# Eight buffers instead of four for the streamed weights in the last stage of a transformer layer

## The chip, the cores and the metric

One Trainium2 chip, all 8 of its cores. Each core runs the same program on its own half of one of the four sequences. The time is the device time of the slowest core, in microseconds (us). In the views, PE is TensorE (its matmuls), PEld its weight loads, DVE is VectorE, ACT is ScalarE, POOL is GpSimd and SP is SyncE. SPq, POOLq and so on are the instruction queues of these engines, out of which DMAs are issued too.

## The reference

`x` is `[4, 2048, 2048]`. The layer is attention and then a feed-forward block, each behind a layer norm and added to `x`. What is computed in the stretch that the change touches is the second half of the feed-forward block:

```python
h = value * jax.nn.silu(gate)        # [4, 2048, 8192]
h = _bitlinear(h, w_out)             # h rounded to -127..127 per row, w_out [2048, 8192] to -1, 0, 1
return residual + h
```

`_bitlinear` rounds the activation by its row's largest value and the weight by its mean absolute value, then multiplies. So the last product is, for each core, `[1024, 8192] x [8192, 2048]` on small whole numbers held as bf16, followed by a scale per row and the addition of the residual.

## The kernel before

The program is a row of blocks with a full barrier between two of them (`fence_block`: SP waits for every counter). The blocks are: constants, projections, attention, the first part of the feed-forward, the gate and value product (`p5_gv`), the rounding and transposing of `w_out` into a DRAM scratch `TOUT` (`p6_tout`), and at last `p7_out2`, the product with `w_out`.

`TOUT` holds the ternary `w_out`, transposed, in bf16 as `[16, 64, 128, 128]`: 16 blocks of 128 output columns, 64 blocks of 128 rows of the contraction.

`p7_out2` runs three blocks, b = 0, 1, 2. The core's 1024 rows are two halves of four row tiles (`qt` 0 to 3).

- With b = 0 and b = 1 it builds (`bld`): it loads the hidden activation from `HMID`, rounds it on DVE, transposes it on PE and puts it at `AQ2T` in SBUF.
- With b = 1 and b = 2 it multiplies (`mm`) the half that was built in the block before. With b = 2 it only multiplies.

The multiplication goes over `j` (0 to 3, 512 output columns each) and inside it over `oc` (0 to 63, the contraction). One step, `("MM", j, oc)`, is a group of four matmuls of 128x128 by 128x512, one for each `qt`, which add into the four banks of `PS_SC`. The right-hand side is a tile of `TOUT`, 128 partitions by 512 columns of bf16 (128 KB), and it is loaded anew for each group: 256 loads in the block, in pieces of 256 bytes (`tob_load`, L1522 to L1532). With `idx = j * 64 + oc` the tile goes into buffer `idx % 4`, at `TOB + (idx % 4) * 256`, and is announced by semaphore `TSEM[idx % 4]`. SP issues the load as soon as the group `idx - 4`, which read that buffer last, has ended (L1526). PE waits for the semaphore at L1637 and runs the four matmuls at L1642.

After group 63 of a `j`, DVE makes four output tiles, `("yb", j, qt)`: it waits for the group, for a tile of the residual (`AF<-X1scr`, two buffers) and for the store from two steps earlier (two buffers `YB`), and then runs L1604 and L1608. POOL stores each tile (`y<-AF`). The first group of the next `j` waits for `("yb", j, 3)`, since it overwrites the banks.

SP issues everything in one written order: for each `j` the 64 `tob_load`, then the four `x1_load` of that `j`. `x1_load` number `idx2` waits for `yb` number `idx2 - 2` (L1538), so the third and fourth of a `j` wait until this `j`'s first two output tiles are made, and the 64 loads of the next `j` stand behind them.

With b = 1 one transpose step stands ahead of every fourth group, and one `HMID` load ahead of every four `tob_load`.

SBUF from 32768 on (in columns of 4 bytes) holds the work buffers of this stage: `HM2` 32768, `AQN` 36352 and 43776 (256 columns each), `TOB` 36608, `X1B7` 37632, `XH` 38656, `YB` 39680, the rounding buffers `ZP7` 40704 to 43776. What lies at 44032 to 45056 is read no more by then.

Of the kernel before, what the change touches and what calls it, by code (L numbers as in the profile page):

```python
# [30 lines left out]
class Prog:  # L31
# [1418 lines left out]
    def p7_out2(self):  # L1450
# [7 lines left out]
        TOB = 36608  # L1458
# [3 lines left out]
        gp_done = self.cnt["GP"]  # L1462
        st_done = self.cnt["ST"]
        TSEM = ["H0", "H1", "S0", "S1"]

        for b in range(3):
            bld = b <= 1
            mm = b >= 1
            self.fence_block(f"f_p7_{b}")
            c0 = dict(self.cnt)  # L1470
            pe_prog, dv_prog, ac_prog = [], [], []
# [30 lines left out]
            PEn = {op: c0["PE"] + i + 1 for i, op in enumerate(pe_prog)}  # L1502
# [3 lines left out]
            with nc.Block(f"p7_{b}") as blk:  # L1506
                @blk.sync
                def _(sy):
                    if b == 0:
                        sy.wait_ge(self.sems["GP"], gp_done)  # L1510
                        sy.wait_ge(self.sems["ST"], st_done)

                    def hm2_load(k):
                        qt, oc16 = k // 16, k % 16
                        i = b * 4 + qt
                        if k >= 4:
                            sy.wait_ge(self.sems["DV"], DVn[("rnd", k - 4)])
                        self.dma(sy, self.af(HM2 + (k % 4) * 512, 512),
                                 self.HMID.ap()[i * 128:(i + 1) * 128,
                                                oc16 * 512:(oc16 + 1) * 512],  # L1520
                                 f"L{k % 4}")

                    def tob_load(j, oc):
                        idx = j * 64 + oc
                        if idx >= 4:
                            sy.wait_ge(self.sems["PE"], PEn[("MM", (idx - 4) // 64,  # L1526
                                                            (idx - 4) % 64)])
                        vsrc = bass.AP(self.TOUT, (j * 4) * 1048576 + oc * 16384,
                                       [[128, 128], [1048576, 4], [1, 128]])
                        self.dma(sy, self.bap(2 * (TOB + (idx % 4) * 256),  # L1530
                                              [[128, 4], [1, 128]]),
                                 vsrc, TSEM[idx % 4])  # L1532

                    def x1_load(j, qt):
                        i = (b - 1) * 4 + qt
                        idx2 = j * 4 + qt
                        if idx2 >= 2:
                            sy.wait_ge(self.sems["DV"], DVn[("yb", (idx2 - 2) // 4,  # L1538
                                                            (idx2 - 2) % 4)])
                        self.dma(sy, self.af(X1B7 + (idx2 % 2) * 512, 512),  # L1540
                                 self.X1scr.ap()[i * 128:(i + 1) * 128,
                                                 j * 512:(j + 1) * 512],
                                 f"X{idx2 % 2}")

                    if bld and mm:
                        for j in range(4):
                            for kk in range(16):
                                hm2_load(j * 16 + kk)
                                for o4 in range(4):
                                    tob_load(j, 4 * kk + o4)  # L1550
                            for qt in range(4):
                                x1_load(j, qt)
                    elif bld:
                        for k in range(64):
                            hm2_load(k)
                    else:
                        for j in range(4):
                            for oc in range(64):
                                tob_load(j, oc)
                            for qt in range(4):  # L1560
                                x1_load(j, qt)

                @blk.vector
                def _(v):
                    rp_feed, rp_flush = self.rp_pipe(v, ZP7, 512)
                    for op in dv_prog:
# [26 lines left out]
                        else:  # L1593
                            rp_flush()
                            _, j, qt = op
                            i = (b - 1) * 4 + qt
                            idx2 = j * 4 + qt
# [17 lines left out]
                @blk.tensor  # L1615
                def _(te):
                    for op in pe_prog:
                        if op[0] == "T":
                            k = op[1]
                            qt = k // 16  # L1620
                            qtg = b * 4 + qt
                            te.wait_ge(self.sems["DV"], DVn[("rnd", k)])
                            if k >= 2:
                                te.wait_ge(self.sems["AC"], ACn[("evac", k - 2)])
                            psb = (self.PS_C if k % 2 == 0
                                   else self.PS_D).ap().bitcast(BF16)
                            for sub in range(4):
                                _l = te.transpose(psb[:, sub * 128:(sub + 1) * 128],
                                                  self.bap(2 * AQN[k % 2] + sub * 128,
                                                           [[1, 128]]),  # L1630
                                                  self.C_idb.ap())
                            _l.then_inc(self.inc("PE", 1), 1)
                        else:
                            _, j, oc = op
                            idx = j * 64 + oc
                            qtg0 = (b - 1) * 4
                            te.wait_ge(self.sems[TSEM[idx % 4]],  # L1637
                                       c0[TSEM[idx % 4]] + 16 * (idx // 4 + 1))
                            if oc == 0 and j > 0:
                                te.wait_ge(self.sems["DV"], DVn[("yb", j - 1, 3)])  # L1640
                            for qt in range(4):
                                _l = te.matmul(  # L1642
                                    self.PS_SC.ap()[:, qt * 512:(qt + 1) * 512],
                                    self.bap(2 * AQ2T + oc * 1024 + (qtg0 + qt) * 128,
                                             [[1, 128]]),
                                    self.bap(2 * (TOB + (idx % 4) * 256), [[1, 512]]),
                                    start=(oc == 0), stop=(oc == 63))
                            _l.then_inc(self.inc("PE", 1), 1)

# [86 lines left out]
```

## Time and profile before

| | us |
|---|---|
| median of the two runs | 7420.96 |
| the two runs | 7306.04 and 7535.88 |
| the profiled execution | 7303.48 |
| its span on the slowest core | 7301.9 |

The views are all of the profiled execution and of core 0, the slowest. Its times count from the first instruction, so the last instruction stands at 7301.9. "Idle before" is the time in which an engine stood still ahead of an instruction, and what follows the arrow is what ended the wait. PEclk or the granted clock is TensorE's clock as a share of 2.4 GHz; 0.50 is 1.2 GHz.

### The profile page before, as it was taken

What the parts mean: (1) busy time and instruction counts of PE and PEld (TensorE: products, weight loads), DVE (VectorE), ACT (ScalarE), POOL (GpSimd) and SP (SyncE); (2) the same over time, 40 slices, a digit from 0 to 9 for tenths busy, and PEclk for the clock granted to TensorE, in tenths of its full rate; (3) what the DMA queues carried; (4) which work ended last, traced back from release to release, by engine and by line L of the source; (5) the groups of instructions that cost most, each with busy time, mean ns of one, the idle gap of its engine ahead of it and who ended that gap; (6) DMA issues with size and microseconds to landing.
All of it is one profiled execution on the core that took longest, in us unless ns stands there. A gap on an engine that the chain in (4) does not pass through costs nothing. (4 is left out here: it accounts for less than half of the span.)

```text
span 7301.9 us, 63207 instructions; the slowest of 8 cores (7249.2 to 7301.9 us)
## 1 busy us (share of the span) xinstructions
PE 4948.8 (68%) x21575; PEld 2384.2 (33%) x21894; DVE 2250.0 (31%) x2790; ACT 1501.2 (21%) x2439; POOL 367.1 (5%) x620
## 2 busy tenths in 40 slices
PE   1666329997898866686767783488888863336776
PEld 1222114443343333332433331234443432212222
DVE  4100260001101123102232213645555546673300
ACT  4555420000000012101222200222222223310000
POOL 0111000000111100000000000000000000000000
PEclk9887659998998977787888886699999985558899
DMA  6899612111101121212111112433333339835555
GB/s 225 281 322 318 207 58 62 55 48 47 35 33 44 41 64 51 68 60 76 52 47 45 41 59 80 166 123 130 130 130 125 116 119 271 212 103 131 134 122 129
DMA packets 665414, 832.70 MB, mean 114 GB/s; under 512 B 434960, under 2 KB 518032, under 8 KB 608144
## 3 DMA queue, kind: packets, MB, share of 16 engines
q1 hardware_dynamic: 468368, 501.45, 23.0%
q0 software_dynamic: 49792, 268.47, 10.6%
q10 hardware_dynamic: 146944, 58.73, 3.0%
q8 instruction: 184, 3.01, 0.2%
q14 instruction: 126, 1.03, 0.0%
HBM read 702.66 MB, written 125.83 MB: 113 GB/s over the span
## 5 line engine op out<-in xcount | busy, mean ns | idle before, releaser
L1285 PE MATMUL PS_SC<-AF 128*128 128x512 bf16 x2048 | 802.4, 392 | 8.4 <-PEq L1209 1.4
L1279 PE MATMUL PS_SC<-AF 128*128 128x512 bf16 x1929 | 757.7, 393 | 60.0 <-PEq L1209 60.0
L904 PE MATMUL PS_C<-AF 128*128 128x512 f32 (+3 forms) x768 | 406.0, 619 | 324.7 <-ACT AF L984 322.2
L653 PE MATMUL PS_D<-AF 128*128 128x512 bf16 x2257 | 531.0, 394 | 139.3 <-ACT AF L673 136.5
L1642 PE MATMUL PS_SC<-AF 128*128 128x512 bf16 x2002 | 524.5, 411 | 101.6 <-DMA AF<-TOUT 64.6
L653 PE MATMUL PS_C<-AF 128*128 128x512 bf16 x2258 | 528.2, 393 | 89.6 <-ACT AF L673 64.4
L748 PE MATMUL PS_C<-AF 128*128 128x512 bf16 x1506 | 341.9, 385 | 151.1 <-DVE AF L723 149.5
L179 ACT ACTIVATE AF<-AF 128x2048 f32<-128x2048 f32 x192 | 366.4, 1909 | 264.5 <-DMA AF<-wgv 170.8
L653 PEld LDWEIGHTS PS_D<-AF 128*128 128x128 bf16 x2304 | 231.4, 101 | 433.5 <-issue 181.9
L871 PE MATMUL PS_SC<-AF 128*128 128x512 f32 (+1 forms) x640 | 316.7, 632 | 71.1 <-DMA AF<-Qscr 48.6
L616 DVE CAST AF<-AF 128x2048 bf16<-128x2048 f32 x32 | 39.2, 1226 | 1025.4 <-PE PS_D L653 997.1
L653 PEld LDWEIGHTS PS_C<-AF 128*128 128x128 bf16 x2304 | 230.6, 101 | 381.5 <-issue 129.1
L1021 PE MATMUL PS_C<-AF 128*128 128x512 f32 x512 | 248.7, 648 | 132.0 <-DMA AF<-wo 132.0
L748 PE MATMUL PS_D<-AF 128*128 128x512 bf16 x1505 | 334.8, 379 | 1.6
L1642 PEld LDWEIGHTS PS_SC<-AF 128*128 128x128 bf16 x2048 | 200.0, 104 | 400.8 <-issue 253.6
L537 PE MATMUL PS_C<-C_idb,AF 128*128 128x128 bf16 x384 | 56.2, 300 | 389.5 <-DVE AF L496 359.8
L1279 PEld LDWEIGHTS PS_SC<-AF 128*128 128x128 bf16 x2048 | 206.2, 101 | 309.1 <-issue 95.4
L1244 DVE SCALAR_TENSOR_TENSOR AF<-AF,V_sgv 128x2048 bf16<-128x2048 f32 x128 | 301.0, 2352 | 13.4
L924 DVE TENSOR_TENSOR PS_SC<-PS_SC,AF 128x256 f32<-128x256 f32 x128 | 55.4, 433 | 783.4 <-PE PS_SC L871 693.7
L1285 PEld LDWEIGHTS PS_SC<-AF 128*128 128x128 bf16 x2048 | 205.7, 100 | 244.1 <-issue 29.5
L968 ACT ACTIVATE AF<-PS_SC,TMP 128x256 f32<-128x256 f32 (+7 forms) x128 | 156.2, 1220 | 584.5 <-DVE TMP L943 500.9
L1256 DVE SCALAR_TENSOR_TENSOR AF<-PS_SC,C1c,AF 128x512 f32<-128x512 f32 x128 | 96.1, 751 | 556.5 <-ACT AF L1323 540.6
(160 smaller groups left out, 5594.3 us busy)
## 6 DMA issues: line engine op xcount, KB each, us to landing
AF<-wgv POOLq DMA_DIRECT2D x128, 1024.0 KB, 8.4
AF<-wgv SPq DMA_DIRECT2D x128, 1024.0 KB, 4.9
AF<-wout POOLq DMA_DIRECT2D x64, 1024.0 KB, 7.7
AF<-wout SPq DMA_DIRECT2D x64, 1024.0 KB, 7.6
AF<-TOUT SPq DMA_DIRECT2D x512, 128.0 KB, 2.9
AF<-wo SPq DMA_DIRECT2D x128, 256.0 KB, 6.2
HMID<-AF POOLq DMA_DIRECT2D x128, 256.0 KB, 2.6
TOUT<-AF ACTq DMA_DIRECT2D x128, 256.0 KB, 6.2
```

What stands on the lines that cost most here:

```text
L179: sc.activation(buf, buf, ACT.Abs, accum_out=self.PARTS.ap()[:, k:k + 1]).then_inc(self.inc("CR", 1), 1)
L653: _pe_last = te.matmul(ps, self.bap(2 * wb[h % 2] + c * 128, [[1, 128]]), self.bap(2 * xb + c * ncols + grp * 512, [[1, 512]]), start=(c = ...
L748: _pe_last = te.matmul(ps, self.bap(2 * xb + c * ncols + tk * 128, [[1, 128]]), self.bap(2 * (wv_ + c * 256), [[1, 512]]), start=(c == 0 a ...
L871: _l = te.matmul(self.PS_SC.ap()[:, ck * 512:ck * 512 + n], self.af(QB0 + (h % 2) * 512 + qt * 128, 128), self.af(KB0 + (h % 2) * 2048 + c ...
L904: te.matmul(self.PS_C.ap()[:, qlo * 128:512], self.af(VB0 + (h % 3) * 2048 + kt * 128, 128), self.af(PTB0 + (kt % 2) * 512 + qlo * 128, 51 ...
L968: sc.activation(self.af(PB0 + (h % 2) * 8192 + qt * 2048, rng), self.PS_SC.ap()[:, 0:rng], ACT.Exp, bias=self.TMP.ap()[:, 4 + qt:5 + qt], ...
L1021: _pe_last = te.matmul(ps, self.af(AVT + c * 512 + qt * 128, 128), self.af(WOB + c * 512, 512), start=(c == 0), stop=(c == 15))
L1244: v.scalar_tensor_tensor(self.bap(2 * (NTB + (g % 2) * 1024), [[1, 2048]]), w, self.V_sgv.ap()[:, 1:2], m1, ALU.is_gt, ALU.subtract).then_ ...
L1256: self.vbar(v, v.scalar_tensor_tensor(hm, psv, self.C1c.ap()[:, qt:qt + 1], self.af(SGB + (qt % 2) * 512, 512), ALU.mult, ALU.mult))
L1279: te.matmul(psv, self.bap(2 * AQ1T + c * 1024 + qt * 128, [[1, 128]]), self.bap(2 * (TT0 + mp * 8192) + c * 512, [[1, 512]]), start=(c == ...
L1285: _l = te.matmul(psg, self.bap(2 * AQ1T + c * 1024 + qt * 128, [[1, 128]]), self.bap(2 * (TT0 + mp * 8192 + 4096) + c * 512, [[1, 512]]), ...
L1642: _l = te.matmul(self.PS_SC.ap()[:, qt * 512:(qt + 1) * 512], self.bap(2 * AQ2T + oc * 1024 + (qtg0 + qt) * 128, [[1, 128]]), self.bap(2 * ...
```

## The change

With b = 2 the tiles of `TOUT` go through eight buffers instead of four. The four new ones lie at `TOB2` = 44032, and use the semaphores `L0` to `L3`, which with b = 2 no other load uses. Buffer, semaphore, the group that SP waits for and the count that PE waits for all follow from `NS`, which is 4 with b = 1 and 8 with b = 2. With b = 1 nothing changes; no instruction is added or taken away with b = 2 but for four waits of SP, which the loads 4 to 7 no longer have.

```diff
@@ p7_out2
         TSEM = ["H0", "H1", "S0", "S1"]
+        TOB2 = 44032
+
+        def tobo(s):
+            return TOB + s * 256 if s < 4 else TOB2 + (s - 4) * 256
 
         for b in range(3):
             bld = b <= 1
             mm = b >= 1
+            TS_Q = TSEM if b == 1 else TSEM + ["L0", "L1", "L2", "L3"]
+            NS = len(TS_Q)
...
                     def tob_load(j, oc):
                         idx = j * 64 + oc
-                        if idx >= 4:
-                            sy.wait_ge(self.sems["PE"], PEn[("MM", (idx - 4) // 64,
-                                                            (idx - 4) % 64)])
+                        if idx >= NS:
+                            sy.wait_ge(self.sems["PE"], PEn[("MM", (idx - NS) // 64,
+                                                            (idx - NS) % 64)])
                         vsrc = bass.AP(self.TOUT, (j * 4) * 1048576 + oc * 16384,
                                        [[128, 128], [1048576, 4], [1, 128]])
-                        self.dma(sy, self.bap(2 * (TOB + (idx % 4) * 256),
+                        self.dma(sy, self.bap(2 * tobo(idx % NS),
                                               [[128, 4], [1, 128]]),
-                                 vsrc, TSEM[idx % 4])
+                                 vsrc, TS_Q[idx % NS])
...
-                            te.wait_ge(self.sems[TSEM[idx % 4]],
-                                       c0[TSEM[idx % 4]] + 16 * (idx // 4 + 1))
+                            te.wait_ge(self.sems[TS_Q[idx % NS]],
+                                       c0[TS_Q[idx % NS]] + 16 * (idx // NS + 1))
...
-                                    self.bap(2 * (TOB + (idx % 4) * 256), [[1, 512]]),
+                                    self.bap(2 * tobo(idx % NS), [[1, 512]]),
```

## Rows read from the trace of the kernel before

**Rows 1.** The page: span, and the chain that ended last, by line.

```profile
span 7301.9 us, 63207 instructions; the slowest of 8 cores (7249.2 to 7301.9 us)
...
DMA AF<-TOUT 2%; PE PS_SC L1642 2%; DMA y<-AF 0%; DVE AF L1604 0%; DVE AF L1608 0%; DMA AF<-X1scr 0%; SPq L147 0%; SPq L1526 0%; POOLq L1506 0%; DVEq L154 0%; DVEq L1602 0%; DVEq L1599 0%; POOLq L1672 0%; DVEq L1598 0%; SPq L1538 0%
```

**Rows 2.** Stretches (us), line L1642 only, one per `j` of the last block.

```profile
core 0: us, PE busy (x) PEld busy (x), PEclk, DMA share, GB/s
6969.07:7041.84 72.77, 62.87 (x251) 23.20 (x256) 0.96 0.52 119
7052.00:7124.71 72.71, 62.27 (x251) 22.91 (x256) 0.97 0.52 119
7135.55:7207.70 72.15, 61.08 (x251) 22.95 (x256) 0.98 0.52 121
7217.80:7287.77 69.97, 60.15 (x251) 23.00 (x256) 0.98 0.53 124
sum 287.60, PE 246.37 PEld 92.06; mean PE 61.59 PEld 23.01
```

**Rows 3.** Gaps and tail: busy PE, PEld, DVE, ACT, POOL; then as in rows 2.

```profile
7041.84:7052.00 10.16, 0.00 (x0) 0.03 (x1) 5.09 (x8) 0.00 (x0) 1.62 (x3) 0.74 0.62 181
7124.71:7135.55 10.84, 0.00 (x1) 0.03 (x1) 5.09 (x8) 0.00 (x0) 1.62 (x3) 0.68 0.62 178
7207.70:7217.80 10.10, 0.00 (x2) 0.03 (x1) 5.09 (x8) 0.00 (x0) 1.62 (x3) 0.64 0.60 182
7287.77:7301.90 14.13, 0.00 (x1) 0.00 (x0) 5.10 (x8) 0.00 (x0) 2.16 (x4) 0.67 0.32 111
```

**Rows 4.** Who waited for whom in the last block: PE's, then SP's queue.

```profile
PE PS_SC L1642 <- DMA AF<-TOUT: 55.5, 77, 17.5
PE PS_SC L1642 <- DVE AF L1608: 31.1, 3, 10.8
...
SPq L1526 <- PE PS_SC L1642: 177.1, 236, 6.2
```

**Rows 5.** The loads of `TOUT` in the last block: issue ns, time to landing.

```profile
L147 SPq DMA_DIRECT2D AF<-TOUT x256: 359/359/1432, 6966.5 to 7283.2; - x128
...
DMA to landing us min/median/max: 2.1/3.0/5.3
```

**Rows 6.** The matmuls of line L1642, ns min/median/max.

```profile
L1642 PE MATMUL PS_SC<-AF x2002: 376/379/635, 6522.9 to 7287.4; 128*128 128x512 bf16 x182
```

**Rows 7.** The chain in order of time: start, us, what.

```profile
6969.07 7.44 PE PS_SC L1642 x20
...
7052.00 6.08 PE PS_SC L1642 x16
...
7058.15 3.67 DMA AF<-TOUT
...
7061.95 1.97 PE PS_SC L1642 x8
...
7135.55 4.42 PE PS_SC L1642 x12
...
7217.80 2.72 PE PS_SC L1642 x6
...
7284.16 3.63 PE PS_SC L1642 x16
```

**Rows 8.** PE alone in a stretch of the projections, about 1200 us in.

```profile
1200.00:1250.00 50.00, 49.79 (x229) 1.00 0.22 65
```

**Rows 9.** The DMA queue of SP in the last block.

```profile
q1 hardware_dynamic: 137472, 37.77, 48.6%
```

**Rows 10.** Timeline at the end of the first `j`: SP, POOL, PE.

```profile
7036.77 8.42 SPq L147 DMA_DIRECT2D AF<-X1scr  x4
...
7045.28 20.82 SPq L147 DMA_DIRECT2D AF<-TOUT  x15
7045.38 0.54 POOL L147 DMA_DIRECT2D y<-AF  x1 [0.77 <-DVE AF L1608]
...
7052.00 7.79 PE L1642 MATMUL PS_SC<-AF 128*128 128x512 bf16 x23 [10.18 <-DVE AF L1608]
...
7052.81 0.15 PEld L1642 LDWEIGHTS PS_SC<-AF 128*128 128x128 bf16 x1 [0.28 <-issue]
7053.24 0.15 PEld L1642 LDWEIGHTS PS_SC<-AF 128*128 128x128 bf16 x1 [0.28 <-issue]
```

**Rows 11.** Timeline at the second end: four loads of SP, the late `X1scr`.

```profile
7125.86 0.55 DVE L1604 TENSOR_SCALAR AF<-AF,ST_a,ST_b 128x512 f32<-128x512 f32 x1 [74.01 <-DMA AF<-X1scr]
...
7129.06 2.45 SPq L147 DMA_DIRECT2D AF<-TOUT  x4
```

## The prediction

> **What bounds the kernel now.** I read the page first. The span is 7301.9 us on the slowest core, the cores end between 7249 and 7302, and the chain that ended last puts only some 2% on the loads of `TOUT` and 2% on the matmuls of L1642 [rows 1]. The change lies in the last block alone (b = 2), so the first question is how long that block is and what its parts are. The stretches by `j` answer it: the matmuls of the four `j` take 72.8, 72.7, 72.2 and 70.0 us, 287.6 us together [rows 2]. Between them lie three gaps of 10.2, 10.8 and 10.1 us, and behind the last a tail of 14.1 us [rows 3]. Each `j` is 64 groups of four matmuls (256 weight loads in the rows; five matmul records of each stretch are missing).
>
> The second question is how long a `j` would take if nothing were late. The last 16 matmuls of the block follow each other without a break: 3.63 us [rows 7]. One matmul lasts 0.379 us from start to end [rows 6], so they start (3.63 - 0.379) / 15 = 0.217 us apart, and a group takes 4 x 0.217 = 0.867 us. A `j` of 256 matmuls would take 255 x 0.217 + 0.38 = 55.6 us. It takes 70 to 73. So 14 to 17 us of each are something else.
>
> The third is what. The waits name it: PE waited for `AF<-TOUT` 77 times, 55.5 us, of which 17.5 are the one wait at the block's start; 38.0 us in 76 waits are left [rows 4]. This counts from the end of the last matmul; a matmul that follows without a break starts 0.379 - 0.217 = 0.162 us before the one ahead of it has ended, so each wait costs the stream 0.162 us more: 38.0 + 76 x 0.162 = 50.3 us. The rest of the excess is the start of each `j`, below, and many waits too short to be named.
>
> Why is a load late? With four buffers SP waits for group idx - 4 before it issues load idx. From there PE has three groups in hand, 3 x 0.867 = 2.60 us. A load lands 3.0 us after its issue in the median, between 2.1 and 5.3 [rows 5]. The chain shows this loop: a load of 3.67 us, eight matmuls, and again a load [rows 7]. SP itself isn't the limit: it stood waiting for PE at L1526 in 177 us of the block [rows 4]. Nor are the DMA engines: SP's queue used 48.6% of their time for 37.77 MB [rows 9]. So the block is bound by the latency of a load against four buffers.
>
> **The change, step by step.**
>
> 1. *More lead.* With eight buffers, load idx is issued when group idx - 8 has ended, and PE has seven groups in hand, 7 x 0.867 = 6.07 us. The longest landing is 5.3 us [rows 5], so at the present latencies no load is late, and the longest hold-up of SP at an issue (1.43 us instead of 0.36 [rows 5]) fits on top of a median load: 3.0 + 1.1 = 4.1 us.
>
> 2. *Does the latency hold?* In the steady state SP issues one load for each finished group, so the rate of issue becomes PE's, one per 0.867 us, instead of 287.6 / 256 = 1.12 us now. The engine time of a load: 48.6% of 335 us is 163 us for 37.77 MB, that is 4.3 us for a MB and 0.57 us for the 0.131 MB of a load [rows 9]. So the engines would be busy 0.57 / 0.867 = 66% with these loads, not 49%. SP needs 2.45 us for four loads without a wait between, (2.45 - 0.36) / 3 = 0.70 us from one to the next, with the median issue of 0.36 us as the last one's [rows 5, 11], also below 0.867. Latency grows somewhat; it may double and still fit into 6.07 us. Bounds: nothing late at all (0 us), or the landings come no faster than now (1.12 us each, the whole gain lost). Nearer are the rows on free engine and queue time; I take 1 us of late loads over the block.
>
> 3. *What is left of a `j`.* The first matmuls of each run at half the clock (1.2 GHz), since PE stood for 10 us or more before: weight loads at 7052.81 and 7053.24, 0.43 us apart [rows 10]. This stays, as the gaps stay. Its price by the chain [rows 7]: 20 matmuls in 7.44 us, where 19 x 0.217 + 0.38 = 4.50 would do, 2.94; 16 in 6.08 against 3.63, 2.45; 12 in 4.42 against 2.76, 1.66; 6 in 2.72 against 1.46, 1.26. Together 8.3 us. So the four `j` take 4 x 55.6 + 8.3 + 1 = 231.7 us, and 287.6 - 231.7 = 55.9 us go.
>
> 4. *The clock.* The 0.217 us is what full clock gives, and the sum needs it at a PE that never rests. In the projections PE was busy 49.8 of 50 us at a granted clock of 1.00, that is 2.4 GHz, while all eight cores ran the same stage [rows 8]. So I take 0.217. The Trainium skill has a rule against this, in TensorE: Matmul & The Clock Gate (Part 1: The HAM clock gate): once three cores of a die run dense matmuls, the whole die is held to 13/16 of the clock. By that rule a matmul would take 0.217 x 16/13 = 0.267 us and the four `j` some 282 us, an estimate from that page, and nearly the whole gain would be gone. The trace doesn't agree with it in the projections, with 1.00 granted.
>
> 5. *The gaps between two `j`.* SP's order is the same: the third and fourth `x1_load` wait for this `j`'s output tiles, and the next `j`'s loads stand behind them, from 7045.28 on in the first gap [rows 10]. The gap is ended by DVE's fourth output tile at L1608 (31.1 us in three waits [rows 4]), and this by the stores of `y` out of two buffers. Two things move. First, all loads of a `j` are issued up to eight groups ahead, so the first `x1_load` goes out some 8 x 0.867 = 6.9 us before the last group ends; in the second gap it was late [rows 11], and the gap 10.84 instead of 10.13, the mean of the others [rows 3]. That is 0.7 us gained. Second, SP now issues eight loads in the gap without a wait instead of four, in the time in which POOL's `y` stores are under way (7045.38 [rows 10]). Four more loads are 4 x 0.57 = 2.3 us of all engines. If a store had to stand behind them all, each of three gaps would be 2.3 us longer, 7 us together; if it finds the engines free, nothing. I take 0.7 each, 2 us, since the stores go through a queue of their own and most of the extra loads are issued after them.
>
> 6. *Start and tail.* PE's first group waits for the first load, as before. The tail of 14.1 us [rows 3] is output tiles and stores, as before. With b = 1 nothing changes, and no other block does.
>
> Sum: 55.9 + 0.7 - 2 = 54.6 us less. The profiled execution took 7303.48, so 7249 us, -0.75%. It is close to the faster of the two runs shown (7306.04); the other, 7535.88, lies 3.1% above, and the median of 7420.96 is the mean of both. Core 1 ends at 7293.9 and gains like core 0, so core 0 stays the slowest or nearly.
>
> **The rivals.**
>
> *A. The loads slow down with their number.* What speaks for it: pieces of 256 bytes, eight cores at once, landings of up to 5.3 us already. Against it: half of the engine time is free, and SP can issue loads 0.70 us apart. If half of the waiting stays, the time is 7303.5 - 27 = 7276 us; if the landings keep their pace of 1.12 us, 7303 to 7310 with the longer gaps.
>
> *B. The clock gives way in part.* With PE at work without a rest, some of its matmuls run at the lower level, 0.43 us apart instead of 0.217 [rows 7, 10]. Each costs 0.21 us, so 54.6 / 0.21 = 260 of them, a quarter of the block's 1024, undo the gain: 7303 us. Against it stands the row at 1.00 [rows 8]. This is the shape that the rule of the page on the clock gate, named above, would give here; by its figure the time would be 7300, an estimate.
>
> *C. Slower: PE falls to the lower level for the whole block.* It decides from the same 260 matmuls on. If all run so, the four `j` take 1024 x 0.43 = 440 us instead of 287.6, 152 us more, and the time is 7303.5 + 152 = 7456 us, slower by 2.1%. For it speaks only that the clock was low at the start of each `j`, for 6 to 20 matmuls. Against it: with all its waits PE was granted 0.96 to 0.98 in the four `j` [rows 2], and the change makes it rest less.
>
> *D. The change does nothing* because a wait on the path is another one: then 7303. The waits by name leave little room for it.
>
> **How the numbers follow.** Forecast, 7235 to 7265 by its own bounds (58 us gained at most, 45 with the longest gaps and some late loads, and a few us between executions: the profiled one and the faster run differ by 2.6): 0.80. A and D: 0.13. B: 0.04. C: 0.03. Time 7249. For the range: low 7232. At the high end A, B and D reach 7310, but the two runs shown differ by 230 us, and a median of two such, 7249 and 7249 x 1.031 = 7474, would be 7361; so the range goes to 7365. A change of under 2%, 146 us, is about what a measurement of this kernel can't tell from none, and no case gains as much: all waits of PE in the block together are less. Faster 0.03 (only if disturbed runs tilt the comparison), same 0.94, slower 0.03.
>
> **What the profile after would show.** Step 1: PE's wait for `AF<-TOUT` in the last block falls from 55.5 to about 18 us, the one at the start. Step 2: the median landing stays below 4 us, SP's queue rises to some 58% of the engines. Step 3: each `j` takes 57 to 59 us. Step 4: PEclk 0.95 or more in each. Step 5: gaps of 10 to 11 us, and no wait for `X1scr`. Wrong would be: landings of 6 us and more, a clock under 0.9, or gaps of 12 us.

## The result, and the profile after

| | before | after |
|---|---|---|
| median of all executions, us | 7445.22 (11) | 7476.39 (12) |
| lowest and highest | 7299.33, 7686.62 | 7242.36, 7682.06 |
| the profiled execution | 7303.48 | 7268.46 |
| ratio after / before | | 0.9925, interval 0.9902 to 0.9948 |

In most executions of either kernel the four cores of one die (0 to 3 or 4 to 7), or of both, get a lower clock for long stretches and end some 80 to 440 us later, so both medians are of such executions, and the ratio compares only the others (three of 7242 to 7252 us against three of 7299 to 7306). By the ratio the kernel became 0.75% faster, and the interval leaves out 1.

The block that was changed is best read on core 0, where the rows of before are from (its span is 7255.8 us; the slowest core was core 1 with 7266.6). First the stretches of the four `j`, line L1642 having become L1648: us, busy PE and PEld, granted clock, DMA share, GB/s. They answer [rows 2].

```profile
6978.50:7036.85 58.35, 58.09 (x251) 25.63 (x256) 0.95 0.65 149
7046.76:7105.12 58.36, 58.09 (x251) 25.63 (x256) 0.95 0.64 151
7115.20:7173.47 58.27, 57.84 (x251) 25.67 (x256) 0.95 0.64 149
7183.80:7241.90 58.10, 57.67 (x251) 25.55 (x256) 0.95 0.65 149
sum 233.08, PE 231.68 PEld 102.47; mean PE 57.92 PEld 25.62
```

287.6 us have become 233.1, and PE is busy in 231.7 of them. The gaps between and the tail, which answer [rows 3] (busy PE, PEld, DVE, ACT, POOL, then as above):

```profile
7036.85:7046.76 9.91, 0.00 (x2) 0.03 (x1) 5.09 (x8) 0.00 (x0) 1.74 (x3) 0.61 0.65 176
7105.12:7115.20 10.08, 0.00 (x1) 0.04 (x2) 5.09 (x8) 0.00 (x0) 1.85 (x3) 0.61 0.70 181
7173.47:7183.80 10.33, 0.00 (x0) 0.03 (x1) 5.00 (x8) 0.00 (x0) 1.62 (x3) 0.60 0.74 182
7241.90:7255.80 13.90, 0.01 (x1) 0.00 (x0) 5.09 (x8) 0.00 (x0) 2.16 (x4) 0.69 0.34 113
```

Who waited for whom, us in total, times, longest: from PE's first matmul in the block to the end, and then SP's own queue over the block. They answer [rows 4].

```profile
PE PS_SC L1648 <- DVE AF L1614: 30.3, 3, 10.3
PE PS_SC L1648 <- DMA AF<-TOUT: 20.1, 1, 20.1
...
SPq L1532 <- PE PS_SC L1648: 107.3, 215, 2.7
```

The loads of `TOUT` in the block, ns of one issue and us to landing (min, median, max), which answer [rows 5]:

```profile
L147 SPq DMA_DIRECT2D AF<-TOUT x256: 359/360/2027, 6975.7 to 7235.1; - x128
...
DMA to landing us min/median/max: 2.2/2.9/5.4
```

SP's queue of DMAs in the block, packets, MB, share of the engines, which answers [rows 9]:

```profile
q1 hardware_dynamic: 137472, 37.77, 59.1%
```

The 76 waits for a late load, 38 us, are gone; the one wait left is that of the block's first load (20.1 us, 17.5 before). A load lands as fast as before, 2.9 against 3.0 us in the median and 5.4 against 5.3 at most, with SP's loads taking 59% of the engines' time instead of 49%. SP was held at an issue for up to 2.0 us (1.4 before) and the lead took that up.

The timeline of the first gap, to be read against [rows 10]: SP issues the two first residual loads 6.4 us before the last group ends (5.1 before), and then eight loads of `TOUT` in 6.34 us while the stores of `y` run.

```profile
7028.30 2.09 SPq L147 DMA_DIRECT2D AF<-TOUT  x3
7030.43 9.78 SPq L147 DMA_DIRECT2D AF<-X1scr  x4
7037.11 0.55 DVE L1610 TENSOR_SCALAR AF<-AF,ST_a,ST_b 128x512 f32<-128x512 f32 x1 [67.99 <-PE PS_SC L1648]
...
7040.30 6.34 SPq L147 DMA_DIRECT2D AF<-TOUT  x8
...
7043.26 0.55 DVE L1610 TENSOR_SCALAR AF<-AF,ST_a,ST_b 128x512 f32<-128x512 f32 x1 [3.44 <-DMA y<-AF]
```

The block's matmuls and gaps together took 318.7 us before (6969.07 to 7287.77) and 263.4 us now (6978.50 to 7241.90): 55.3 us less. The span of core 0 is only 46 us shorter, since this execution reached the block 9 us later, through blocks whose instructions are the same in both kernels.

### The profile page after: what moved, and what is told of

The parts are those of the page before. It is cut to its first block and busy times, and to the rows that moved or that the text cites. A ratio compares the mean times of both kernels' runs of the same rounds, so it can differ in the third digit from the quotient of the medians.

```text
span 7266.6 us, 63522 instructions; the slowest of 8 cores (7189.2 to 7266.6 us)
## 1 busy us (share of the span) xinstructions
PE 4952.6 (68%) x21894; PEld 2391.6 (33%) x21894; DVE 2248.7 (31%) x2790; ACT 1502.2 (21%) x2439; POOL 364.5 (5%) x620
## 5 line engine op out<-in xcount | busy, mean ns | idle before, releaser
L1279 PE MATMUL PS_SC<-AF 128*128 128x512 bf16 x2048 | 804.0, 393 | 61.3 <-PEq L1209 61.3
L1285 PE MATMUL PS_SC<-AF 128*128 128x512 bf16 x2048 | 802.4, 392 | 0.0
L1648 PE MATMUL PS_SC<-AF 128*128 128x512 bf16 x2048 | 508.0, 408 | 58.0 <-DVE AF L1614 30.7
L653 PEld LDWEIGHTS PS_D<-AF 128*128 128x128 bf16 x2304 | 231.7, 101 | 430.6 <-issue 181.5
L1648 PEld LDWEIGHTS PS_SC<-AF 128*128 128x128 bf16 x2048 | 207.1, 104 | 331.4 <-issue 145.5
```

The lines of the kernel that those rows point to most:

```text
L653: _pe_last = te.matmul(ps, self.bap(2 * wb[h % 2] + c * 128, [[1, 128]]), self.bap(2 * xb + c * ncols + grp * 512, [[1, 512]]), start=(c = ...
L1279: te.matmul(psv, self.bap(2 * AQ1T + c * 1024 + qt * 128, [[1, 128]]), self.bap(2 * (TT0 + mp * 8192) + c * 512, [[1, 512]]), start=(c == ...
L1285: _l = te.matmul(psg, self.bap(2 * AQ1T + c * 1024 + qt * 128, [[1, 128]]), self.bap(2 * (TT0 + mp * 8192 + 4096) + c * 512, [[1, 512]]), ...
L1648: _l = te.matmul(self.PS_SC.ap()[:, qt * 512:(qt + 1) * 512], self.bap(2 * AQ2T + oc * 1024 + (qtg0 + qt) * 128, [[1, 128]]), self.bap(2 * ...
```

## The experiments

The theory, L: a load is late when it lands later than the groups in hand last, so the gain is a matter of lead alone. Against it stand T (more loads in flight move more bytes per us) and S (the place of the new buffers, or one semaphore for fewer loads, brought it). Then three runs ask what is left in the last block, and two what set the other multiplying block. The stretches read below are of cores at full clock in the block (matmuls 0.216 us apart where none is late), unless it is said otherwise. The time that a block takes is counted from PE's first weight load in it to its last.

### Five buffers

```diff
-            TS_Q = TSEM if b == 1 else TSEM + ["L0", "L1", "L2", "L3"]
+            TS_Q = TSEM if b == 1 else TSEM + ["L0"]
```

> The changed kernel with five buffers in the last block instead of eight. Theory L (a load is late when it lands later than the groups in hand last): five buffers leave PE four groups, 4 x 0.867 = 3.47 us, against landings of 3.0 us in the median and 5.3 at most, so most waits go and some stay: 59 to 64 us for each j, where four buffers take 70 to 73 and eight take 57 to 58.4. Rival T (the loads were held by the pace at which the transfers go, and eight in flight raise that pace): five buffers give a fifth of the way, 67 to 70 us.

The stretches of the four `j` on core 0, and PE's waits from its first matmul of the first `j` on:

```profile
7258.42:7318.48 60.06, 58.59 (x256) 24.36 (x256) 0.97 0.63 144
7328.92:7389.66 60.74, 58.95 (x256) 25.00 (x256) 0.96 0.62 143
7400.60:7461.38 60.78, 59.09 (x256) 25.06 (x256) 0.96 0.62 145
7472.36:7532.22 59.86, 58.66 (x256) 25.19 (x256) 0.96 0.62 146
```

```profile
PE PS_SC L1648 <- DMA AF<-TOUT: 22.6, 14, 16.8
```

60 to 61 us for each `j`, within what L expects, and far from T's 67 to 70. One buffer more, 0.87 us of lead, took the named waits from 76 (38 us) to 13 (5.8 us). Of the 256 landings on core 0 of the kernel before, 20% lay under the old lead of 2.60 us, 81% under 3.47 and 95% under the 4.33 of six buffers; so the first buffer more clears most of the waits. This execution took 7621 us, with a lower clock on both dies ahead of the block and on four cores in it. The block took 273 to 277 us on the four cores at full clock (275 in the mean), where the kernel before has 313 and the changed one 262.

### Six buffers

```diff
+            TS_Q = TSEM if b == 1 else TSEM + ["L0", "L1"]
```

> The changed kernel with six buffers. Theory L: five groups in hand, 4.33 us, only the slowest landings are late: 57.5 to 59.5 us for each j, so six buffers bring nearly all that eight do. Rival T: in proportion to the number in flight, 62 to 66 us.

The stretches of the four `j` on core 0:

```profile
6927.66:6985.53 57.87, 57.56 (x256) 25.29 (x256) 0.97 0.65 149
6995.76:7054.31 58.55, 57.80 (x256) 25.25 (x256) 0.96 0.64 150
7064.97:7122.88 57.91, 57.54 (x256) 25.05 (x256) 0.97 0.64 147
7133.24:7190.49 57.25, 57.20 (x256) 25.08 (x256) 0.97 0.64 151
```

57.3 to 58.6 us, as L has it: six buffers give nearly what eight give. The block took 263.5 us in the mean of the eight cores against 261.8, and the named waits behind the first came to 1.3 us in 4 on core 0. The execution took 7246 us, as the changed kernel. Both T and any other gain in proportion to the number are out.

### Eight buffers with the lead of four

```diff
-                        if idx >= NS:
-                            sy.wait_ge(self.sems["PE"], PEn[("MM", (idx - NS) // 64,
-                                                            (idx - NS) % 64)])
+                        if idx >= 4:
+                            sy.wait_ge(self.sems["PE"], PEn[("MM", (idx - 4) // 64,
+                                                            (idx - 4) % 64)])
```

> The changed kernel with its eight buffers and eight semaphores, but SP waits for group idx - 4 before it issues load idx, as the kernel before does. Theory L: the lead is that of four buffers, so each j takes 70 to 73 us again and PE's waits for TOUT stay near 55 us. Rival S (the gain came from the place of the buffers or from eight semaphores in the place of four): 57 to 59 us for each j.

The stretches of the four `j` on core 0, then the landings, then the waits from the first matmul on:

```profile
6944.69:7011.27 66.58, 61.38 (x256) 23.17 (x256) 0.97 0.57 128
7022.01:7091.00 68.99, 61.78 (x256) 23.50 (x256) 0.96 0.53 124
7101.93:7168.22 66.29, 60.85 (x256) 23.18 (x256) 0.97 0.56 128
7179.98:7244.48 64.50, 60.47 (x256) 23.17 (x256) 0.96 0.57 132
```

```profile
DMA to landing us min/median/max: 2.1/2.6/5.9
```

```profile
PE PS_SC L1648 <- DMA AF<-TOUT: 37.9, 42, 17.4
```

The gain of the buffers is gone without the lead, so S is out. But 64.5 to 69.0 us is less than the 70 to 73 that I expected. On this core the median landing was 2.6 us instead of 3.0, and its waits fell to 20.5 us in 41 (without the first). Over the block this kernel took 299 to 316 us on the six cores at full clock (308 in the mean), the kernel before 304 to 318 on its eight (313) and the changed one 260 to 263 (262). So the lead is 46 of the 51 us between the last two. The other 5 lie within the spread of the cores; whether eight places have a small part in them is not settled. The two cores that were held to a lower clock in the block (6 and 7, matmuls 0.26 us apart for most of it) took 314 us, hardly more than the others.

### Two sets of banks in the last block

```diff
+            def bank(j, qt):
+                if b == 2 and j % 2 == 1:
+                    return (self.PS_A, self.PS_B, self.PS_C, self.PS_D)[qt].ap()
+                return self.PS_SC.ap()[:, qt * 512:(qt + 1) * 512]
...
                             for oc in range(64):
                                 tob_load(j, oc)
-                            for qt in range(4):
-                                x1_load(j, qt)
+                                if oc in (40, 44, 48, 52):
+                                    x1_load(j, (oc - 40) // 4)
...
-                            if oc == 0 and j > 0:
-                                te.wait_ge(self.sems["DV"], DVn[("yb", j - 1, 3)])
+                            if oc == 0 and j > (b - 1):
+                                te.wait_ge(self.sems["DV"], DVn[("yb", j - b, 3)])
```

Matmul and output tile take their bank from `bank`, and the residual tiles lie in four buffers in the place of `HM2` with b = 2.

> The changed kernel, and in the last block the odd j add into the other four banks (PS_A to PS_D), so that PE doesn't wait for the output tiles of the j before; the residual tiles get four buffers and are loaded during the j, after groups 40, 44, 48 and 52, so that SP never stands at an output tile. If the three gaps (10.2 us each) and three of the four starts at half the clock (2.2 us each on the mean) are what is left in the block besides PE's own work, the matmuls of the block run in one stretch of 4 x 55.6 + 3 = 225 to 227 us, and the block is 36 to 38 us shorter than that of the changed kernel: 0.9925 of the kernel before becomes 0.987 to 0.988. If the stores of y and the residual loads delay loads of TOUT beyond seven groups, or the clock sinks at a PE without any rest, 5 to 20 us of it don't come.

The whole stretch of matmuls on core 0, and its `TOUT` loads:

```profile
6933.70:7167.92 234.22, 225.15 (x1024) 99.63 (x1024) 0.99 0.78 174
```

```profile
L149 SPq DMA_DIRECT2D AF<-TOUT x256: 359/360/2954, 6930.9 to 7161.1; - x128
...
DMA to landing us min/median/max: 2.2/3.6/6.6
```

234 us in one stretch instead of 263 with gaps: 29 us, not 37. On the six cores at full clock the block took 229 to 237 us (232 in the mean). PE's own work is the 225 that was expected; the other 9 us on core 0 are late loads, 8.8 us in 10 named waits behind the first. The gaps had kept the residual loads and the stores of `y` away from the matmuls. Now they share the stretch, the engines are busy 78%, a landing takes 3.6 us in the median and up to 6.6, and SP was held up to 2.95 us at one issue of `TOUT` and up to 3.76 us at one of a residual tile. On core 6 of this execution the granted clock was lower in this block (us, PE busy, granted clock, DMA share, GB/s):

```profile
7310.00:7360.00 50.00, 50.00 (x195) 0.83 0.62 151
```

195 matmuls in 50 us are 0.256 us each, where [rows 8] has 229 records. The block took 269 us there and on core 7. That isn't to be set against the 262 of the changed kernel, whose cores all had full clock in this block. The nearest cores at a lower clock for most of the block are those of the run with five buffers (2, 3, 6 and 7), with 299 to 307 us. So the gain of the two sets of banks seems to hold at the lower clock too, but the changed kernel itself was not seen there. This kernel is judged by its block alone.

### Eight buffers in the block b = 1 too

```diff
-            TS_Q = TSEM if b == 1 else TSEM + ["L0", "L1", "L2", "L3"]
+            TS_Q = TSEM + (["N0", "N1", "N2", "N3"] if b == 1
+                           else ["L0", "L1", "L2", "L3"])
```

> The changed kernel, with eight buffers in the block b = 1 too (four semaphores of their own). In the kernel before this block takes 429 us from PE's first to its last instruction, where 4 x 55.6 us of matmuls and 64 transposes of 0.6 us would be 261. If the lead of the TOUT loads matters there as well, through SP, whose HMID loads stand behind the TOUT loads in the written order and go out four groups (3.5 us) earlier with eight buffers: 30 to 120 us shorter, and 0.975 to 0.99 of the kernel before. If DVE's rounding chain (four operations and their waits, some 2.6 us for each tile, one tile for each four groups) or PE's own order holds the block, 0 to 15 us, and the ratio stays at 0.991 to 0.9925.

The block b = 1 from PE's first weight load to its last (core 0; us, then busy PE, PEld, DVE, ACT, POOL, granted clock, DMA share, GB/s), and under it its waits, first in the kernel before:

```profile
6522.11:6951.00 428.89, 292.31 (x1252) 123.87 (x1279) 161.20 (x291) 38.73 (x65) 6.48 (x12) 0.83 0.53 131
```

```profile
DVE AF L215 <- DMA AF<-HMID: 146.2, 45, 7.6
...
PE PS_C L1628 <- DVE AF L202: 130.6, 32, 18.3
...
PE PS_SC L1642 <- DMA AF<-TOUT: 9.2, 19, 1.0
```

Then with eight buffers (core 0):

```profile
6924.95:7239.16 314.21, 248.73 (x1278) 114.02 (x1279) 161.00 (x291) 38.73 (x65) 6.52 (x12) 0.92 0.74 179
```

```profile
DVE AF L217 <- DMA AF<-HMID: 82.3, 44, 7.1
...
PE PS_C L1637 <- DVE AF L204: 61.1, 16, 14.8
```

115 us shorter, at the upper end of what was expected: on the eight cores 304 to 314 us, 308.6 in the mean, where the changed kernel has 412 to 432, 425.4 in the mean, 117 more. All eight cores had full clock in this block. In the block before, PE hardly waited for `TOUT` by name (9.2 us in 19 waits), and still the depth of the `TOUT` buffers set it. The waits form a chain: PE for the rounded tile of DVE, DVE for `HMID`, and the `HMID` load stood in SP's order behind a `TOUT` load that waited for PE. The granted clock rose from 0.83 to 0.92 as the pauses went. By this run alone the chain is argued; the next run tests it.

### The HMID load one step earlier, four buffers

```diff
+                        hm2_load(0)
                         for j in range(4):
                             for kk in range(16):
-                                hm2_load(j * 16 + kk)
+                                if j * 16 + kk < 63:
+                                    hm2_load(j * 16 + kk + 1)
                                 for o4 in range(4):
                                     tob_load(j, 4 * kk + o4)
```

> The changed kernel (four TOUT buffers with b = 1, eight with b = 2), with one thing moved in SP's order of the block b = 1: the HMID load of tile k + 1 stands ahead of the four TOUT loads of step k, one step earlier than before. It asks by which way eight buffers shortened that block from about 425 to about 308 us. If by the HMID loads, which stood behind TOUT loads that waited for PE: with four TOUT buffers and this order the block falls by more than half as much, to 300 to 365 us. If by the TOUT loads themselves, it stays at 405 to 430 us.

The same block on core 0, and its waits:

```profile
6511.23:6867.24 356.01, 264.20 (x1279) 110.94 (x1280) 160.76 (x291) 38.79 (x65) 6.53 (x12) 0.92 0.64 157
```

```profile
PE PS_C L1636 <- DVE AF L202: 53.8, 4, 16.4
...
PE PS_SC L1650 <- DMA AF<-TOUT: 43.9, 81, 1.8
```

356 us on core 0, 345 to 363 on the eight, 352 in the mean: 73 of the 117 us come from this order alone, and the place of the `HMID` load is shown as the main way. What PE then waits for is late `TOUT` loads, 43.9 us in 81 waits, just as in the last block. So four buffers hurt b = 1 twice, first through SP's order and, with that mended, through their own lead: the 43 us that are left to the run with eight buffers, whose `HMID` loads have the same lead as here. This execution took 7200 us.

Its last block is that of the changed kernel, and tells something of the latency. The landings on core 0 took 3.6 us in the median there (2.2 to 6.3), with SP's queue at 60% of the engines; in the changed kernel's execution it was 2.9 us at 59%. Still no load was late, and the block took 262 us as there. So one and the same block has medians from 2.9 to 3.6 us in different executions, where the runs with the engines at 78% have 3.5 to 4.2, and the lead of eight buffers takes the difference up.

### All of it

Eight buffers in both blocks and two sets of banks, once with the residual loads on SP's queue and once on ACT's, which has nothing to do with b = 2:

```diff
+                    if b == 2:
+                        for j in range(4):
+                            sc.wait_ge(self.sems["PE"], PEn[("MM", j, 24)])
+                            for qt in range(4):
...
+                                self.dma(sc, self.af(X1P + (idx2 % NX) * 512, 512),
```

> Both together: eight buffers in both multiplying blocks, and the two sets of banks with four residual buffers in the last. The two lie in different blocks with a barrier between, so the savings add: the time of the run with b = 1 alone less 36 us if the two sets of banks bring what their own run shows.

> Eight buffers in both multiplying blocks, two sets of banks in the last, and there the sixteen residual loads go out from ACT's queue instead of SP's, after group 24 of each j. In the run with them on SP the matmuls of the last block took 234 to 239 us, with 11 to 14 us of late TOUT loads behind residual loads that held SP for up to 3.8 us each. If SP's lost lead is the reason, 225 to 228 us now; if the residual loads' share of the DMA engines is, 232 to 238 us as before. The whole: 54 us of the change, 115 of the block b = 1, 36 to 43 of the last block, 0.970 to 0.973 of the kernel before, if no clock is taken away.

The residual loads differ in their time as well: on ACT they go out after group 24 of a `j`, on SP behind groups 40 to 52. The last block's matmuls, on core 4 with the residual loads on SP and then on core 4 with them on ACT (us, in the first also PE and PEld busy, then granted clock, DMA share, GB/s), and the landings of the latter:

```profile
6849.42:7084.35 234.93, 225.47 (x1004) 99.71 (x1024) 0.99 0.78 174
```

```profile
6829.89:7058.11 228.22, 0.99 0.78 179
```

```profile
L149 SPq DMA_DIRECT2D AF<-TOUT x256: 359/360/1803, 6827.5 to 7051.3; - x128
...
DMA to landing us min/median/max: 2.3/3.6/7.1
```

Over all eight cores, nearly all of them at full clock in this block in both, it took 232 to 239 us with the loads on SP (236 in the mean) and 228 to 239 with them on ACT (232). The named waits for `TOUT` behind the first fell from 10.0 to 6.9 us a core. But the last block of the run with two sets of banks above has the same code as the one with the loads on SP, and it took 232 us with 7.2 us of such waits. So the move to ACT's queue is not shown to gain anything beyond the spread of executions. The 225 to 228 us that were expected if SP's lost lead were the reason came on one core of eight (228), so it is at most a part of it. With no residual load on its queue SP was still held up to 1.8 us at a load on core 4 and up to 4.7 on core 0, and the latest landings were 7 to 10 us, beyond the lead of 6.07. What makes those landings late was taken away by no run.

The savings of the blocks add, as expected. With the residual loads on SP, six dies kept a mean granted clock of 0.83 or more on every core, and their cores ended at 7098 us in the mean; those of the kernel before, run beside it, ended at 7291. That is 192 us less, where the three blocks' savings of 51, 117 and 26 us make 194. One execution of this kernel took 7163 us, with all cores at such a clock. The kernel with the loads on ACT took from 7096 us on, 0.9733 of the kernel before, interval 0.9676 to 0.9789 (0.970 to 0.973 expected). So it beats the kernel before, and by the two intervals the changed one too.

## Why the prediction was right and wrong

**The mechanism and the sum: right.** Steps 1 and 3 came out within 2 us: a `j` at 58.1 to 58.4 us (57 to 59 forecast), 54.5 us gone of the matmuls' 287.6 (55.9 forecast), starts at half the clock as before. PE's wait for `TOUT` fell to the one at the block's start (20.1 us, about 18 forecast). The forecast of the whole was 7249 us and -0.75%. The ratio is 0.9925, 55 us less where 54.6 were forecast. Executions without the lower clock took 7242, 7248 and 7252 us, and the profiled one 7268. That the whole agrees to a fraction of a us is partly luck, since the parts were off by 1 to 2 us each way.

**Step 2, the latency: right.** The median landing is 2.9 us, and the engine share came to 65% inside a `j` (66% forecast). Rival A is out for this change. It appears in a small form where the gaps are gone too, with medians of 3.5 to 4.2 us on the cores at full clock.

**Step 5, the gaps: the size was off.** I took 2 us for stores of `y` behind extra loads and 0.7 us gained from the residual load. The three gaps went from 31.1 to 30.3 us together [rows 3]: 0.8 us shorter, not 1.3 longer. The second gap lost 0.76 us, and the others moved by 0.25 us either way. The stores' wait of DVE is as long as before (15.4 against 15.5 us), so the eight loads didn't delay them.

**The time and the range: wrong.** The step that failed is what turns the sum into a median: "The profiled execution took 7303.48, so 7249 us", and for the high end "a median of two such, 7249 and 7249 x 1.031 = 7474, would be 7361; so the range goes to 7365". The forecast put the lower clock at nothing in the time, and in the range at one execution of two, whose cost the mean of both then halves. Measured, nine of the twelve executions of the changed kernel had it, at 7328 to 7682 us, up to 6% above the others. So the middle of the twelve is itself such an execution, and the median is 7476, 227 us above the time forecast. The term of 3.1% came out by the number (7474 against 7476); that it hit so closely is luck, since it was one draw out of 1 to 6%. What was mis-sized is its share, and with it the halving. The two times of before were too few to tell: the kernel before has 7405 to 7687 us in eight of its eleven. Nothing in the record says that the change makes the difference, and the ratio isn't moved by it.

**Step 4, the clock: right for the profiled execution, too wide as a sentence on the kernel.** [Rows 8] shows one core of one execution that didn't have it. The same stretch in the run with five buffers, core 0 (us, PE, granted clock, DMA share, GB/s):

```profile
1200.00:1250.00 50.00, 50.00 (x192) 0.81 0.14 43
```

192 matmuls in 50 us instead of 229 records, at a granted clock of 0.81. By the Trainium skill (TensorE: Matmul & The Clock Gate, Part 1: The HAM clock gate) dense matmuls on three or more cores of a die bring it to 13/16, which is 0.8125; this trace agrees, and that of [rows 8], with the same program on the same number of cores, doesn't. I weighed the rule for the block alone, set it aside by one trace, and didn't ask whether the second run, 230 us higher, was the rule at work in the blocks ahead. In the run with five buffers, whose code is the same up to the last block, core 0 came to the block b = 1 at 6821 us instead of 6528, and in the run with eight buffers in b = 1 at 6925 us. In the last block of the latter all eight cores had full clock again, and it took 260 to 263 us as in the changed kernel, though the execution took 7622. So the time went ahead of the blocks that the change is about.

Rival B was some matmuls 0.43 us apart with PE at work without a rest. In the changed kernel no weight loads of the block are that far apart later than 12 us into a `j`, on any core. What some cores of other runs had in the last block was the form of step 4, matmuls 0.26 us apart at a granted clock near 0.81, and not that of B, under which I had put it. In the run with five buffers, core 6 took 69.7 us for its first `j`, with PE busy in 69.5 of them.

```profile
7237.94:7307.67 69.73, 69.46 (x256) 28.07 (x256) 0.79 0.54 124
```

There much of the gain is gone: cores 2, 3, 6 and 7 of that run took 299 to 307 us for the block, against 314 on the two cores at a lower clock with the lead of four buffers, where full clock gives 275 against 308. The changed kernel's trace has no such core in the block. Rival C (half the clock through the block) appeared in no run. Rival D is out.

## What to carry to other kernels

Compare the time from a load's issue to its landing with the work in hand while it flies, here buffers less one times the group's time. Most of the gain comes where the lead passes the common landing: five buffers brought 38 of the 51 us, six nearly all. A queue with one written order passes a shallow buffer's wait on to every load behind it: look for loads that stand behind a waiting one, even where nobody waits for the shallow buffer by name. And before a range is given for a median, ask what most executions do, not only the profiled one.

## What I had not expected

- The block b = 1 lost 117 us to the four buffers, over twice what the changed block lost, with 9.2 us of named waits for them.
- The median landing held at 3.0 and 2.9 us on core 0 while the engines' share inside a `j` went from 52% to 65%, and rose to 3.5 to 4.2 us at 78%. The share alone doesn't set it: in the last block of the changed kernel it is 2.9 to 3.2 us over the cores, in two other executions of the same block 3.0 to 3.6.
- In nine of twelve executions of the changed kernel a die had a lower clock. In a trace with it the granted clock was 0.81 in dense matmuls, and it came and went: with five buffers, cores 2 and 3 had it for most of the last block, cores 0 and 1 of the same die not at all.
